# Sums of two score tables on GpSimd: one broadcast operation, or sixteen with a scalar operand

## The reference

```python
q = (x @ Wq).reshape(b, t, H, 2, DK)              # H = 4 heads
sim1 = einsum('bthd,hkd->bthk', q1, keys[:, :, 0])  # 128 scores each
sim2 = einsum('bthd,hkd->bthk', q2, keys[:, :, 1])
s1, i1 = top_k(sim1, 8); s2, i2 = top_k(sim2, 8)
all_scores = s1[..., :, None] + s2[..., None, :]
final_scores, pk_idx = top_k(all_scores, 8)        # index = i1 * 128 + i2
hidden = silu(x . e_down[index]) * relu(final_scores)
out = sum(hidden * e_up[index])
```

## Time and profile before

| | |
|---|---|
| median of 3 runs | 4386.55 us (4381.77 to 4388.78) |
| the profiled execution | 4390.64 us |
| its span between first and last instruction | 4388.9 us |
| PE busy in the span | 3856.2 us |
| DVE busy | 2624.5 us |
| ACT busy | 1997.4 us |
| GpSimd busy | 901.4 us |

### The profile page before, as it was taken

How to read it: one execution, slowest core, us unless ns; L and a number is a source line. 1 busy time by engine, 2 the same in 40 slices (tenths; PEclk the granted TensorE clock), 3 DMA queues, 4 the chain that set the end, 5 groups by cost and what they waited for, 6 DMA issues and landing times. The chain is left out here.

```text
span 4388.9 us, 76482 instructions
## 1 busy us (share of the span) xinstructions
PE 3856.2 (88%) x26248; PEld 3265.7 (74%) x26248; DVE 2624.5 (60%) x6005; ACT 1997.4 (46%) x5211; POOL 901.4 (21%) x743
## 2 busy tenths in 40 slices
PE   6776999999898876999999999799989998887791
PEld 5555888889776765788888888688878886666671
DVE  7887999999576336555555555444433334666533
ACT  6885666666323433444434443333333333775140
POOL 1113323233001331000000000122223332001245
PEclk9997999999998997999999999899999998998695
DMA  2001000000001013111111111422232221002244
GB/s 71 18 12 46 1 0 0 0 0 1 27 22 46 0 51 140 46 40 40 40 37 35 40 40 39 115 70 68 66 105 73 72 74 43 13 14 67 73 135 130
DMA packets 148634, 209.45 MB, mean 48 GB/s; under 512 B 20576, under 2 KB 87424, under 8 KB 147968
## 3 DMA queue, kind: packets, MB, share of 16 engines
q1 hardware_dynamic: 141488, 187.14, 13.9%
q0 software_dynamic: 6864, 18.75, 1.5%
HBM read 178.18 MB, written 27.66 MB: 47 GB/s over the span
## 5 line engine op out<-in xcount | busy, mean ns | idle before, releaser
L1241 ACT ACTIVATE peer_tab<-peer_sims 128x128 f32<-128x128 f32 x1024 | 305.7, 394 | 0.0
L1248 POOL TENSOR_TENSOR peer_tab<-peer_sims 128x2048 f32<-128x2048 f32 x64 | 247.2, 3882 | 276.8 <-ACT peer_sims L1225 248.4
L1296 DVE SCALAR_TENSOR_TENSOR peer_tab<-peer_tab,peer_th 128x2048 f32<-128x2048 f32 x128 | 298.4, 2374 | 2.6 <-ACT peer_tab L1241 2.3
L1313 PE MATMUL bank<-ident,peer_tab 128*128 128x128 f32 x2048 | 247.8, 275 | 23.7 <-DVE peer_tab L1296 23.7
L1313 PEld LDWEIGHTS bank<-ident,peer_tab 128*128 128x128 f32 x2048 | 234.5, 142 | 37.1 <-DVE peer_tab L1296 24.6
L1363 PE MATMUL bank<-peer_wd,peer_hh 128*128 128x256 f32 x1024 | 246.4, 384 | 2.5 <-DVE peer_hh L1354 2.5
L1336 PE MATMUL bank<-peer_hT,peer_wg 128*128 128x256 f32 x1024 | 244.4, 382 | 0.0
L651 DVE TENSOR_TENSOR moe2a_b<-moe2a_a,moe2a_spread 128x512 f32<-128x512 f32 x104 | 78.4, 754 | 235.9 <-ACT moe2a_a L625 232.7
L1336 PEld LDWEIGHTS bank<-peer_hT,peer_wg 128*128 128x128 f32 x1024 | 196.2, 192 | 26.6
L1363 PEld LDWEIGHTS bank<-peer_wd,peer_hh 128*128 128x128 f32 x1024 | 185.2, 190 | 30.7 <-DVE peer_hh L1354 7.5
L651 DVE TENSOR_TENSOR moe2b_b<-moe2b_a,moe2b_spread 128x512 f32<-128x512 f32 x96 | 68.0, 708 | 233.1 <-ACT moe2b_a L625 232.7
(11 more groups left out here) (503 smaller groups left out, 10996.3 us busy)
## 6 DMA issues: line engine op xcount, KB each, us to landing
mha_wo<-mha_wo SPq DMA_DIRECT2D x128, 256.0 KB, 2.6
moe2b_spread<-moe_shares SPq DMA_DIRECT2D x48, 256.0 KB, 3.1
moe2a_spread<-moe_shares SPq DMA_DIRECT2D x40, 256.0 KB, 3.5
m_y_rows<-moe_y SPq DMA_DIRECT2D x79, 128.0 KB, 1.7
att_ctxT<-in_ctxT_dram SPq DMA_DIRECT2D x32, 256.0 KB, 2.6
lin_ctxT<-in_ctxT_dram SPq DMA_DIRECT2D x16, 256.0 KB, 2.6
mem_ctxT<-in_ctxT_dram SPq DMA_DIRECT2D x16, 256.0 KB, 2.6
mem_ctx<-in_ctx_dram SPq DMA_DIRECT2D x16, 256.0 KB, 2.9
```

The source lines that it names most:

```text
L1241: i = nc.scalar.activation(tab[g][h][:, b * P:(b + 1) * P], sims[:, g, 1, h, :], ACT.Identity, bias=sims[:, g, 0, h, b:b + 1])
L1248: nc.gpsimd.tensor_tensor(out=tab[g][h][:].rearrange("p (a b) -> p a b", b=P), in0=sims[:, g, 1, h, :].unsqueeze(1).broadcast_to([P, NB, P ...
L1296: nc.vector.scalar_tensor_tensor(out=tab[g][h][:], in0=tab[g][h][:], scalar=th[:, g, h:h + 1], in1=tab[g][h][:], op0=ALU.is_ge, op1=ALU.mu ...
L1313: i = nc.tensor.matmul(TB[n % 2][:, j * P:(j + 1) * P], tab[g][h][:, blk * P:(blk + 1) * P], core.ident[:], start=(j == 0 and h == 0), sto ...
```

## The change

`sums_pool` makes the same sums with sixteen tensor_scalar operations in place of one tensor_tensor: operation b writes columns 128 b to 128 b + 127, reads the 128 scores of the second table, and takes column b of the first table as a scalar per partition. An increment of the semaphore `passed` stands between the waits and the first of them. The last of the sixteen signals DVE.

```diff
     def sums_pool(pool, t, g, h):
         sims_wait(pool, t, g)
         sums_free(pool, t, g)
-        nc.gpsimd.tensor_tensor(out=tab[g][h][:].rearrange("p (a b) -> p a b", b=P),
-                                in0=sims[:, g, 1, h, :].unsqueeze(1).broadcast_to([P, NB, P]),
-                                in1=sims[:, g, 0, h, 0:NB].unsqueeze(2).broadcast_to([P, NB, P]), op=ALU.add).then_inc(sum_pool, 1)
+        pool.sem_inc(passed, 1)
+        for b in range(NB):
+            i = nc.gpsimd.tensor_scalar(tab[g][h][:, b * P:(b + 1) * P], sims[:, g, 1, h, :], sims[:, g, 0, h, b:b + 1], None, ALU.add)
+        i.then_inc(sum_pool, 1)
```

## The result

The changed kernel takes 4564.69 us (median of 4 runs, 4560.5 to 4565.33) against 4384.75 us (4 runs, 4381.77 to 4388.78): a ratio of 1.0407 with a 95% interval of 1.0392 to 1.0422. The direction was forecast, the size was not: 12 us forecast, 180 us measured, far above the range.

A forecast was written before the change was run, and what follows sets the result against it. PE was taken to bound the peer stage; 9.4 us over 14 tiles plus 2.6 at the start made 12 us, forecast 4398.5 us against a median of 4386.55, range 4379 to 4446.

The forecast's parts named there:

- slack in group 0: Peer stage, group 0: xn is done at 757.87, PE's weight load of the transposes starts at 759.60, 1.73 us later.
- The price X: Start-to-start spacing of GpSimd's 128-column tensor_scalar operations in the sums: taken as 0.40 us, range 0.26 to 0.50.
- Rival (c): GpSimd's sums: each operation fetches its scalar anew, spacing 0.47 us or more; 4446 us at 0.50, 4494 at 0.60; chance 0.15.
- The holds: Time DVE's masks, products and small operations hold GpSimd's sums off before head 3's mask: 8.3 us a group.
- The delay doesn't add up with group 1's: Peer's steady tiles: group 1 late by about as much against its own 4.4 us, so only group 0's 0.67 us counts.
- the prediction's own formula: Group 0, steady tiles: head 3 is ready 32X + 8.3 us after GpSimd's start; PE waits beyond 18.7 + 1.73.
- The start: Start of the peer stage, where PE waits outright for the masks: +3.0 us, 0.4 given back, so +2.6 us.

The follow-up runs named there:

- the kernel with group 0 alone: Against the kernel before, sixteen tensor_scalar operations make group 0's tables only; group 1 keeps its one tensor_tensor a table: 4504.48 us, ratio 1.0266.
- with group 1 alone: Against the kernel before, sixteen tensor_scalar operations make group 1's tables only; group 0 keeps its one tensor_tensor a table: 4544.77 us, ratio 1.0351.

## Why the prediction was wrong in its size

- **What bounds the kernel before** was read rightly: PE, with 1.73 us of slack in group 0. Everything that kept GpSimd short enough left the time at 4379 to 4388 us.
- **The price X failed.** 0.579 us against 0.40 and a range to 0.50. It was put together from a tensor_scalar of two columns with a constant and a column price of 0.0016 us taken across two other operations, a cast and a select. The form's own column price is 0.0025 us (0.11 us more over 126 columns), and the scalar from memory, for which the value taken held nothing, is 0.086 us more; together 0.20, where X was missed by 0.18. Rival (c) had the scalar's mechanism and 0.50 to 0.60 for X; the measured X lies between the two, and the measured time far beyond its 4446 to 4494 us, for the reason given below under the delay.
- The Trainium skill (GPSIMD Engine Reference, section 7, Performance pitfalls for Q7 kernels) has a read command at some 102 cycles, an estimated 0.085 us; the constant in place of the scalar saved 0.086, so the size agrees, and that the scalar is such a read command no run shows. The Trainium skill's section 4.1 of the same reference (Engine selection) calls work on one input roughly line-rate; for this operation the runs don't agree: 0.0025 us a column is an estimated three cycles at that reference's 1.2 GHz, and the two-input form costs less (0.997 - 0.357 = 0.64 us for 384 columns, 0.0017 each).
- **The holds were right in sum, in part by luck.** Two groups at 8.3 us were forecast, 16.3 us a tile were measured. But without the seventh mask, which the prediction did not count, the measured holds of a group are some 7 us (7.2 for group 1's; 6.8, 25.3 - 18.5, in the kernel with group 0 alone): a mask holds a sum for about 1.8 us and not 2.1. The small operations do stay shut out while a mask runs, and with full masks cut short the loss was gone.
- **"The delay doesn't add up with group 1's" failed.** It holds where GpSimd has a gap between the groups. The two groups' chains share one engine: with the measured 16.3 us of holds and 5.9 of norm, 64X + 16.3 + 5.9 exceeds 48.29 from X = 0.41 on, hardly above the 0.40 that I took. From there each 0.01 us costs 0.64 us a tile and not 0.32. With the X measured, the prediction's own formula gives 32 x 0.579 + 8.3 - 20.43 = 6.4 us a tile, some 4480 to 4490 us. The changed kernel lost 59.33 - 48.29 = 11.0: the 4.6 us more, some 64 us over 14 tiles, are this step. The kernel with group 0 alone, in which GpSimd has the gap, lost 6.7 us a tile.
- **The start and the end.** The start was put at +2.6 us; the norm after it starts 8.0 us later. The end of the stage, where the last tiles' sums run after the last norm, was put at nothing, and is 14.7 us longer.
- **PE's clock was left out.** In the changed kernel PE waits 4.00 us for the table at 704.09; then the granted clock is at its lower level, 1.2 GHz, and the table takes 3.67 us in place of 1.91:

```profile
704.00:707.50 3.50, 3.41 (x16) 3.42 (x17) 2.96 (x11) 0.60 (x1) 3.50 (x5) 0.50 0.01 2
```

  Not every such wait ends so: in the kernel with group 0 alone tables take from 1.96 to 3.67 us after waits of 3.4 to 3.6. In the steady tiles of the changed kernel the rows show no cost, as GpSimd's operations and the norm follow each other without a wait for PE; with group 1 alone it is 1.7 of the 9.7 us a tile.

## What to carry to other kernels

An engine that is idle two thirds of the time is still one engine: before its work is made dearer, sum all that it does in a period, the time that others hold it off and the waits of its own loop, and compare that with the period, besides the slack of each chain. Price a new operation by its own form, or take the range as wide as the forms differ: here tensor_scalar and tensor_tensor differ by 1.6 at the same columns, the other way round than their inputs suggest. On GpSimd, cutting a tensor_tensor into pieces gave VectorE some of its waits back and cost the kernel no time; sixteen tensor_scalars gave them back too, at a price far above the gain.

## What was not expected of the hardware

- A tensor_scalar on GpSimd is dearer than a tensor_tensor at 128 columns with the same two operands from memory: 0.579 against 0.357 us from start to start.
- GpSimd and DVE do not always take turns. In the earlier trace rows mask and sum alternate, and with the small tensor_scalars each mask waits for one at most. But a mask that came 0.06 us after the start of a row of tensor_tensors waited for the whole row, two of 3.6 us or eight of 1.0 us. In the kernel before, a product that came 0.61 us after the first of two sums waited for that one alone. Which of them gets in, and why, stays open: that it hangs on the moment of the request was not tried.
